# A decoder block's routed experts: the first tile gathered by whole rows and turned on TensorE, the weights' sums moved behind it, the last tiles scattered in halves

## The reference

```python
gate_logits = jnp.einsum('bsh,he->bse', x, gate_w)        # 8 experts
top_vals, top_idx = jax.lax.top_k(gate_logits, 2)
probs = jax.nn.softmax(top_vals, axis=-1)
onehot = jax.nn.one_hot(top_idx, 8, dtype=x.dtype)
w_e = jnp.einsum('bsk,bske->bse', probs, onehot)
expert_out = jnp.einsum('bsh,eho->bseo', x, expert_w)     # 1024 x 1024 each, f32
out = jnp.einsum('bseo,bse->bso', expert_out, w_e)
```

## Time and profile before

| what | value |
|---|---|
| executions shown | 1143.48, 1146.24 and 1150.12 us; median 1146.24 |
| profiled execution, span | 1141.4 us (the page gives no other time for it) |
| PE busy | 1016.4 us, 89% |
| DVE, ACT, POOL busy | 570.2, 403.1 and 481.5 us |
| mean granted clock of TensorE | 0.947 of full |
| bytes moved | 120.25 MB, mean 105 GB/s |

### The profile page before, as it was taken

The page is one execution under the profiler, slowest core; times in us unless marked ns, Lnnn a source line. Parts: engine busy times, 40 slices in busy tenths (PEclk is TensorE's granted clock), DMA queues, the critical chain, the costliest instruction groups (busy, mean ns, idle before and its releaser), DMA issues. The chain is left out here.

```text
span 1141.4 us, 13560 instructions
## 1 busy us (share of the span) xinstructions
PE 1016.4 (89%) x3534; PEld 532.5 (47%) x3535; DVE 570.2 (50%) x1661; ACT 403.1 (35%) x1142; POOL 481.5 (42%) x662
## 2 busy tenths in 40 slices
PE   6788789899998869799746999999999999999995
PEld 6686445455544435434423444444444444444442
DVE  5645679898788788987986111111111111111111
ACT  2435788797777327757730000000000000000000
POOL 3843666566665101006614433333344444443331
PEclk9878899998899989999976999999999999999998
DMA  8410111010000321002597346373737346373332
GB/s 303 139 59 0 48 47 38 25 70 1 1 1 1 134 99 64 1 1 92 222 381 264 87 133 165 74 220 74 220 74 220 76 123 183 84 227 78 74 74 37
DMA packets 38463, 120.25 MB, mean 105 GB/s; under 512 B 6220, under 2 KB 9351, under 8 KB 38408
## 3 DMA queue, kind: packets, MB, share of 16 engines
q1 hardware_dynamic: 25592, 79.77, 19.0%
q0 software_dynamic: 12816, 39.86, 16.0%
HBM read 82.91 MB, written 36.70 MB: 105 GB/s over the span
## 5 line engine op out<-in xcount | busy, mean ns | idle before, releaser
L2017 PE MATMUL bank<-T,X 128*128 x1184 | 508.8, 592 | 0.0
L2017 PEld LDWEIGHTS bank<-T,X 128*128 128x128 f32 x1184 | 225.1, 190 | 283.6 <-issue 283.6
L2079 DVE TENSOR_SCALAR X<-bank,col_p 128x512 f32<-128x512 f32 x37 | 27.8, 751 | 401.6 <-PE bank L2017 401.6
L2045 ACT ACTIVATE X<-bank,col_p 128x512 f32<-128x512 f32 x37 | 25.4, 687 | 495.5 <-PE bank L2017 466.7
L1970 POOL DMA_INDIRECT X<-x_nrm,col_s x156 | 150.3, 964 | 71.6 <-issue 46.9
L1979 POOL DMA_INDIRECT out_dram<-X,col_d x37 | 60.0, 1622 | 263.3 <-DVE X L2079 255.2
L821 ACT ACTIVATE M<-X,T 128x256 bf16<-128x256 f32 x200 | 98.6, 498 | 0.5
L451 POOL TENSOR_TENSOR T<-T 128x8 f32<-128x8 f32 x216 | 88.1, 408 | 16.3
L640 PE MATMUL bank<-nat,T 128*128 128x512 f32 x128 | 73.6, 710 | 6.6 <-ACT X L809 3.7
L460 POOL TENSOR_TENSOR rs<-ve,neg_half 128x4 f32<-128x4 f32 x36 | 37.3, 1036 | 79.4 <-DVE ve L960 78.9
L217 POOL TENSOR_TENSOR late<-late,neg_half 128x1 f32<-128x1 f32 x32 | 17.8, 557 | 112.0 <-DVE late L213 112.0
(11 more groups left out here) (333 smaller groups left out, 1457.9 us busy)
## 6 DMA issues: line engine op xcount, KB each, us to landing
T<-in_L_ffn_expert_w_dram SPq DMA_DIRECT2D x8, 4096.0 KB, 17.7
out_dram<-X SPq DMA_DIRECT2D x17, 512.0 KB
M<-in_x_dram SPq DMA_DIRECT2D x16, 512.0 KB, 7.2
X<-in_x_dram SPq DMA_DIRECT2D x16, 512.0 KB, 6.8
x_nrm<-H SPq DMA_DIRECT2D x16, 512.0 KB, 3.5
T<-in_ctx_dram SPq DMA_DIRECT2D x9, 512.0 KB, 3.6
X<-x_nrm,col_s POOLq DMA_INDIRECT x156
X<-in_ctx_dram SPq DMA_DIRECT2D x4, 512.0 KB, 7.0
```

The source lines that it names most:

```text
L2017: mm = nc.tensor.matmul(bank[2 * u + n][:, :], xgt[u][:, k, :], Tf[:, ds(odd * D + (k * N + n * BANK), BANK)], start=(k == 0), stop=(k == ...
```

## The change

The first slot's rows come by one indirect DMA of 128 whole rows, issued in the first block with indices (row_0) taken from bank TOKEN. Its rows are put into plain order by ACT and DVE (`in_order`, in the room yv[0]), turned by eight transposes on PE into banks 2 and 3, and copied into xgt[0] by ACT and DVE, all in the first block. Six idle-time products stand ahead of the transposes (`keep_busy(0, 6)`). PE's two PROB groups move behind slot 0's products, `weighted` moves from the first block into the second, and the computation of end_i, who, ready_i and odd_i from the second into the first. The seven idle-time products go. The last three slots are each scattered in two indirect DMAs of 128 half rows (2 KB), the first as soon as ACT's half is there. Moved definitions are left out of this diff.

```diff
             def _(pool):
...
+                for u in range(2):
+                    pool.wait_ge(nrm_st[u], B * 16)
+                pool.wait_ge(out_init, NT * 16 + 32)
+                hold(pool, tok_set, 2)
+                nc.gpsimd.indirect_dma_start(out=xg[0], out_offset=None, in_=x_nrm[:, :],
+                                             in_offset=bass.IndirectOffsetOnAxis(ap=row_0[:, 0:1], axis=0)).then_inc(xg_in[0], 16)
...
                 mm.then_inc(r_pe, 1)
+                keep_busy(0, 6)
+                for k in range(KD):
+                    if k == 0:
+                        pe.wait_ge(r_act, 2)
+                    if k == KU:
+                        pe.wait_ge(tok_set, 3)
+                    mm = nc.tensor.transpose(bank[TURNED[k // KU]][:, (k % KU) * P:(k % KU + 1) * P], yv[0][:, k * P:(k + 1) * P], ident[:, :])
+                    if k % KU == KU - 1:
+                        mm.then_inc(r_pe, 1)
...
                 a.activation(e2[:, :], e2[:, :], ACT.Exp).then_inc(r_act, 1)
+                hold(act, xg_in[0], 16)
+                a.copy(in_order[:, 0:KU, :, :], by_parts[:, 0:KU, :, :]).then_inc(r_act, 1)
+                act.wait_ge(r_pe, 5)
+                a.copy(xgt[0][:, 0:KU, :], bank[TURNED[0]][:, :].rearrange("p (k n) -> p k n", k=KU)).then_inc(r_act, 1)
...
                 v.tensor_copy(tok_parts[:, :, 0:SLOTS], ...).then_inc(tok_set, 1)
-                for j in range(2):
-                    weighted(0, j)
+                weigh(dve, v.tensor_reduce(row_f, bank[TOKEN][:, 0:2 * WIDE].rearrange("p (j s) -> p s j", j=2)[:, 0, :], AX.X, ALU.add))
+                v.tensor_scalar(row_0[:, :], row_f, 1.0 / QK, None, ALU.mult).then_inc(tok_set, 1)
                 dve.wait_ge(r_pe, 4)
                 route(v.tensor_scalar(src_i[:, :, :].rearrange("p s c -> p c s"), ...))
+                v.tensor_scalar(end_i[:, :], end, 1.0, None, ALU.add)
...
+                weigh(dve, v.tensor_scalar(odd_i[:, :], who_i[:, :], 1, None, ALU.bitwise_and))
+                hold(dve, xg_in[0], 16)
+                v.tensor_copy(in_order[:, KU:KD, :, :], by_parts[:, KU:KD, :, :]).then_inc(tok_set, 1)
+                dve.wait_ge(r_pe, 6)
+                v.tensor_copy(xgt[0][:, KU:KD, :], bank[TURNED[1]][:, :].rearrange("p (k n) -> p k n", k=KU)).then_inc(xg_tp, 1)
...
-                for u in range(2):
-                    pool.wait_ge(nrm_st[u], B * 16)
-                pool.wait_ge(out_init, NT * 16 + 32)
-                for u in range(IN_FLIGHT):
+                def scatter_halves(j, u):
+                    for n, done in enumerate((y_act, y_dve)):
+                        hold(pool, done, j + IN_FLIGHT + 1)
+                        g.indirect_dma_start(out=out_halves, out_offset=bass.IndirectOffsetOnAxis(ap=col_h[u][:, n:n + 1], axis=0),
+                                             in_=yv[u][:, n * BANK:(n + 1) * BANK], in_offset=None, compute_op=ALU.add).then_inc(y_out, 16)
+
+                for u in range(1, IN_FLIGHT):
                     gather(u, u)
...
                     with pool.If(used > j + 1):
-                        scatter(j, u)
-                        pool.wait_ge(y_out, j * 16 + 16)
+                        scatter_halves(j, u)
+                        pool.wait_ge(y_out, LAST[0] * 16 + 32 * u + 32)
...
                 pe.sem_inc(tile_mm, 1)
+                pe.wait_ge(r_act, 3)
+                products(0, 0)
                 for k in range(2):
                     pe.wait_ge(p_set, k + 1)
                     for t in range(NT):
                         mm = nc.tensor.matmul(bank[PROB][:, 0:3 * WIDE], ...)
                 mm.then_inc(p_mm, 1)
-                dense = ...
-                for i in range(7):
-                    nc.tensor.matmul(bank[0][:, :]..., ident..., dense, start=(i == 0), stop=(i == 6))
-                with pe.Fori(0, ITER) as i:
+                for u in range(1, IN_FLIGHT):
+                    products(0, u)
+                with pe.Fori(1, ITER) as i:
...
                 dve.sem_inc(y_dve, IN_FLIGHT)
-                for u in range(IN_FLIGHT):
+                dve.sem_inc(src_set, 1)
+                for u in range(1, IN_FLIGHT):
                     sources(u, u)
-                weighted(0, 2).then_inc(p_set, 1)
...
-                turned(0, 0, 0)
                 sources(IN_FLIGHT, 0)
+                for k in range(2):
+                    for j in range(3):
+                        ins = weighted(k, j)
+                    ins.then_inc(p_set, 1)
...
                 v.tensor_scalar(dst_i[:, :], dst_f[:, :], -1.0, None, ALU.add)
+                for n in range(2):
+                    v.tensor_scalar(half_i[:, n, :], dst_f[:, LAST[0]:SLOTS], n / 2 - 1.0, 2.0, ALU.add, ALU.mult)
                 dve.wait_ge(p_mm, 1)
                 weigh(dve, v.tensor_reduce(pair_p[:, :], ...))
                 for u in range(IN_FLIGHT):
                     columns(u, u)
                 for u in range(1, LEAD):
                     turned(u, 0, u)
                     sources(u + IN_FLIGHT, u)
```

More of the change, by code:

```diff
@@ L1465, in wait_gated @@
                 eng.wait_ge(gm_done, 2 * (b - 1) + n + 1)
+        ITER = SLOTS // IN_FLIGHT - 1
+        LAST = range(ITER * IN_FLIGHT, SLOTS)
+        xg = [Xf[:, u * D:(u + 1) * D] for u in range(IN_FLIGHT)]
+        xgt = [Xf[:, (3 + u) * D:(4 + u) * D].rearrange("p (k n) -> p k n", k=KD) for u in range(IN_FLIGHT)]
+        xg_blocks = [xg[u].rearrange("p (c k a) -> p c k a", c=QK, k=KD) for u in range(IN_FLIGHT)]
+        xgt_blocks = [xgt[u].rearrange("p k (c b) -> p c k b", c=QK) for u in range(IN_FLIGHT)]
+        x_quarters = x_nrm.rearrange("n (i c) -> (n i) c", i=QK)
+        yv = [Xf[:, (6 + u) * D:(7 + u) * D] for u in range(IN_FLIGHT)]
+        LEAD = IN_FLIGHT - 1
+        col_s = [sb(f"col_s{u}", [P, QK], U32) for u in range(IN_FLIGHT)]
+        col_d = [sb(f"col_d{u}", [P, 1], U32) for u in range(IN_FLIGHT)]
+        col_p = [sb(f"col_p{u}", [P, 1]) for u in range(IN_FLIGHT)]
+        xg_in = [sem(f"xg_in{u}") for u in range(IN_FLIGHT)]
+        src_set, cols_set, xg_tp, y_mm, y_act, y_dve, y_out, w_ready, tile_mm = (sem(n) for n in (
+            "src_set", "cols_set", "xg_tp", "y_mm", "y_act", "y_dve", "y_out", "w_ready", "tile_mm"))
+        out_halves = out.rearrange("n (i c) -> (n i) c", i=2)
+        col_h = [sb(f"col_h{u}", [P, 2], U32) for u in range(IN_FLIGHT)]
+        half_i = small(2, IN_FLIGHT, dt=U32)
+        row_f = small(1)
+        row_0 = sb("row_0", [P, 1], U32)
+        TURNED = (2, 3)
+        by_parts = xg[0].rearrange("p (i k a) -> p k i a", i=QK, k=KD)
+        in_order = yv[0].rearrange("p (k i a) -> p k i a", i=QK, k=KD)
         with nc.Block() as block:
@@ L1928, in _ @@
                                       quarter[:, 0:1], None, ALU.add))
[L1932 to L1946, removed]
+                v.tensor_scalar(end_i[:, :], end, 1.0, None, ALU.add)
+                weigh(dve, v.tensor_tensor(past[:, :, :], iota_slot[:, :].unsqueeze(1).to_broadcast([P, E, SLOTS]),
+                                      end.unsqueeze(2).to_broadcast([P, E, SLOTS]), ALU.is_ge))
+                weigh(dve, v.tensor_reduce(who[:, :], past[:, :, :].rearrange("p e s -> p s e"), AX.X, ALU.add))
+                weigh(dve, v.tensor_scalar(who[:, :], who[:, :], float(E - 1), None, ALU.min))
+                v.tensor_scalar(ready_i[:, :], who[:, :], 1.0, None, ALU.add)
+                weigh(dve, v.tensor_copy(who_i[:, :], who[:, :]))
+                weigh(dve, v.tensor_scalar(odd_i[:, :], who_i[:, :], 1, None, ALU.bitwise_and))
[3 more added lines that the diff above has]
+                v.tensor_copy(xgt[0][:, KU:KD, :], bank[TURNED[1]][:, :].rearrange("p (k n) -> p k n", k=KU)).then_inc(xg_tp, 1)
         with nc.Block() as block:
@@ L2027, in _ @@
                 mm.then_inc(p_mm, 1)
-                dense = ones[:, :].bitcast(BF16).unsqueeze(1).to_broadcast([P, 2, 2 * P])
-                for i in range(7):
-                    nc.tensor.matmul(bank[0][:, :].rearrange("p (a n) -> p a n", a=2), ident[:, :].bitcast(BF16)[:, 0:P], dense, start=(i == 0), stop=(i == 6))
-                with pe.Fori(0, ITER) as i:
+                for u in range(1, IN_FLIGHT):
+                    products(0, u)
+                with pe.Fori(1, ITER) as i:
                     for u in range(IN_FLIGHT):
@@ L2060, in turned @@
                 def turned(j, i, u):
-                    hold(dve, xg_in[u], i * (QK * 16) + QK * 16)
+                    hold(dve, xg_in[u], i * (QK * 16) + (16 if u == 0 else QK * 16))
                     if not isinstance(j, int) or j >= IN_FLIGHT:
@@ L2072, in columns @@
                 def columns(j, u):
-                    v.tensor_copy(col_d[u][:, :], dst_i[:, ds(j, 1)])
+                    if isinstance(j, int) and j in LAST:
+                        v.tensor_copy(col_h[u][:, :], half_i[:, :, u])
+                    else:
+                        v.tensor_copy(col_d[u][:, :], dst_i[:, ds(j, 1)])
```

## The result

The changed kernel takes 1153.34 us (median of 4, 1152.0 to 1155.15), the kernel before 1145.95 beside it (median of 4, 1143.48 to 1150.12): ratio 1.0063, 95% interval 1.0032 to 1.0094. It is slower by 7.4 us. The prediction was 1153.4 with a range of 1147.0 to 1160.0.

A forecast was written before the change was run, and what follows sets the result against it. The experts' products on PE, 508.8 of 1141.4 us, were taken to bound the kernel; 2.2 + 2.25 + 1.8 + 2.3 - 1.4 = +7.15 us on 1146.24 gave 1153.4, range 1147.0 to 1160.0.

The forecast's parts named there:

- rows used to first product: Slot 0's reordering, eight transposes, copy out of PSUM, block seam and PE's value reads before the first product: 5.7 us.
- clock: At the products' start: PE idles around the transposes, so early products run at clock 0.50; +2.25 us, bounds 1.9 and 2.6.
- PROB: Behind slot 0: 32 small products, formerly in PE's waiting time, stand between two slots; +1.8 us, bounds 1.8 and 3.6.
- tail: Behind the last product: ACT's half goes 5 us earlier, leaving only the second half's transfer; -1.4 us, bounds -2.0 and 0.
- Start of the first product: Slot 0's start: earlier gather, but contention, transposes, seam and value reads follow; +2.2 us, bounds -2.4 and +3.9.
- The step with contention: Slot 0's gather beside expert 1's load: data start 2.5 us behind the issue, then 0.52 MB take 3.3 us.
- The lower bound: First product's start if the gather is undisturbed, 1.9 us from end of issue to use: -2.4 us.
- rival 1: Slot 0's gather lands undisturbed by expert 1's load; sum +2.5 us, time 1148.8; chance 17 in 100.
- The new wait: Between PROB and slot 1's products PE waits for DVE's sum, six column copies and turn; +2.3 us, bounds 2.2 and 2.6.
- Rival 2: The clock falls in PE's wait ahead of slot 1, costing 1.65 us more; 1155 to 1157; chance 20 in 100.
- Rival 3: At the kernel's end the halves shorten nothing, the tail being fixed latency; +8.5 us, 1154.8; chance 8 in 100.
- Moves with cover: Gathers for slots 1 and 2, SP's column waits, keep_busy's products and POOL's store waits move; expected covered, POOL's at worst +1.7 us.

The follow-up runs named there:

- the run with the load behind: Changed kernel with expert 1's 4 MB load issued only when slot 0's rows have landed; 1152.04 us, ratio 1.0053.
- four of its variants: Changed kernel with whole scatters, expert 1's load after slot 0's rows, slot 0's turn in the second block, or more idle-time products; copy to end 545.4, 540.1, 542.2, 543.3 us.
- the two runs on the tail: Changed kernel with last three slots scattered whole, tail 13.1 us; kernel before with only the scatter in halves added, tail 11.7 us, ratio 0.9981.

## Why the prediction was right

The working held term by term, with a few sizes off and one bound wrong:

| step | predicted | changed kernel |
|---|---|---|
| gather issued, behind the copy | 1.8 | 1.85 |
| its issue | 1.4 | 1.24 |
| rows used, behind the end of the issue | 6.1 | 6.8 |
| rows used to first product | 5.7 | 5.55 |
| first product against before | +2.2 | +2.65 |
| clock | +2.25 | +2.1 |
| PROB | +1.8 | +1.77 |
| wait for slot 1 | +2.3 | +2.16 |
| tail | -1.4 | -1.7 (1.5 over all profiles) |
| sum | +7.15 | +7.0 |

The clock's 2.1 is what is left of 514.86 us of products when 508.79 of before, 1.77 and 2.16 are taken off. The largest misses, 0.45 at the start and 0.3 at the tail, have opposite signs and cancel; that the sum came out within 0.2 is partly this luck. That the time itself came out within 0.1 is more of it: the medians lie 7.4 us apart, 0.25 more than forecast, and the kernel before came out at 1145.95, 0.29 under the 1146.24 that the forecast started from.

The 4.84 us carried from span to median are two things. Only 2.0 of them lie around an execution's span (1153.31 us against 1151.3 in the changed kernel); the rest is that the profiled execution was the fastest of those shown. As the forecast is the median plus the sum, this does no harm.

*Start of the first product.* The step with contention was right in kind: nothing of the software queue until well after the issue, then half the engines. In the changed kernel it cost 3.3 us, by the run with the load behind. What I had too low is the sum of delay and transfer, 6.1 for 6.8. The lower bound was wrong: an undisturbed gather was priced by a quarter gather, 1.9 us, while 128 whole rows need 3.5. With that, rival 1 starts at 12.1 instead of 10.4 us behind the copy and its +2.5 becomes about +4.2.

*The Trainium skill's* DMA: Bandwidth & Descriptors, section Anatomy of one DMA, gave an estimate of 3.2 us for these bytes. The prediction counted it from the beginning of the issue, and from there the gather took 4.7 us undisturbed and 8.0 beside the load, so the trace does not agree in either case; from the end of the issue the undisturbed one took 3.5. Rival 1, in which the gather slips ahead of the load, did not come true.

*The new wait* was right in place and size; the one-line move of the turn removes 1.7 of its 2.16. *Rival 2*, the fall of the clock, did not happen in the changed kernel's two profiles and did in four of its variants, at 1.7 us each, the price given. So 20 in 100 looks low. The two rows that I took for it, idle stretches of 2.4 and 3.3 us, did not bracket it: falls came behind 2.2. TensorE: Matmul & The Clock Gate of the Trainium skill, section HAM oscillation, describes a kernel whose clock falls behind each wait for a DMA; the waits there are longer than this one. Here a fall followed in four profiles of six.

*Rival 3* fell by the two runs on the tail: the halves are worth 1.5 us in the trace, in either kernel. *Moves with cover* held: no other wait appeared, and 36 slots take 494.68 us where the clock stays up.

## What to carry to other kernels

Before a stage's first transfer is started sooner, look at what lay in its waiting time: here the small products, the block's end, the value loads and the warming of the clock were free only because PE waited for the gathers, and each came due once the wait was to be shorter. Done early again, the sums gave back 3.4 us; but none of the versions with an early first slot came below the kernel before with the halves alone, and the early sums together with the load behind the gather were not tried. Cost a moved step by what is queued behind it on each engine: a wait for sums ahead of the next slot's turn cost 2.2 us, and the order of two lines took most of it away. When an effect is smaller than the runs' scatter, count from a fixed instruction right ahead of the change.

## What the runs showed of the hardware

The end of a block of code waited for POOL's own indirect DMA: drains of 8.25 and 8.51 us, and of 4.93 with the load behind, each until the rows had landed; in the kernel before, with no such DMA under way there, it lasted 0.65. The stage counted from its first copy repeats better than a whole execution: the kernel before with halves gave 532.8 and 532.7 us, the changed one 541.8 and 542.5, while over all profiles that copy itself stood at 606.64 to 619.70 us; what moves the part ahead of it was not looked into. An indirect DMA of 128 rows beside a 4 MB load moved nothing for at least 2.8 us behind the end of its issue and then had half of the engines, 51 packets to 54 in one microsecond. And 26 idle-time products in a row raised the granted clock to 1.00, but behind an idle stretch of 2.6 us it was at 0.50 again before the products began.
